# Other orders and engines for the norms, token sums, weight sums and first quad of an attention-plus-FFN kernel

## What is computed

```python
x = x + attn(layernorm(x))        # (8, 1024, 512)
x = x + ffn(layernorm(x))

# attn
c   = (x @ W_to_kv.T) @ W_compress.T              # 1024 x 64
ch  = layernorm(c) * gamma + beta
q, k, v = ch @ W_q.T, ch @ W_k.T, ch @ W_v.T      # 64 each, rope on q and k
o   = softmax(causal(q @ k.T / 8)) @ v
z   = o @ W_comp2lat.T
out = z @ W_to_kv + z @ W_out_res.T + b_out_res

# ffn
hidden = silu(x @ W1.T) * (x @ W3.T)              # 1024 x 2048
out    = fwht(hidden) @ W2.T                      # back to 512
```

## Time and profile before

| | |
|---|---|
| median of 3 runs | 2152.87 us (2150.15 to 2155.82) |
| the profiled execution | 2155.15 us, span 2153.4 us |
| mean granted clock of TensorE | 0.99 |
| TensorE busy | 2014.3 us, 94% |
| VectorE, ScalarE, GpSimd busy | 70%, 54%, 51% |
| DMA | 312.57 MB, 48.3% of 16 engines |

### The profile page before, as it was taken

The page is one execution under the profiler, slowest core; times in us unless marked ns, Lnnn a source line. Parts: engine busy times, 40 slices in busy tenths (PEclk is TensorE's granted clock), DMA queues, the critical chain, the costliest instruction groups (busy, mean ns, idle before and its releaser), DMA issues.

```text
span 2153.4 us, 32679 instructions
## 1 busy us (share of the span) xinstructions
PE 2014.3 (94%) x11862; PEld 1170.9 (54%) x11862; DVE 1503.4 (70%) x2626; ACT 1166.4 (54%) x1775; POOL 1091.7 (51%) x788
## 2 busy tenths in 40 slices
PE   6889999978999999999999999999999999999998
PEld 3534444445555656555555555556565555556665
DVE  7897878757776686866867687775868668663333
ACT  5866454454554656455555646546564465554443
POOL 2346641476554555455455545545555554555554
PEclk8999999999999999999999999999999999999999
DMA  8656346453464534725347444554347353373332
GB/s 326 221 192 221 122 137 168 140 174 135 123 147 131 174 102 126 181 90 164 111 119 186 133 138 121 129 148 154 122 124 177 99 165 98 113 166 125 116 97 89
DMA packets 267264, 312.57 MB, mean 145 GB/s; under 512 B 181344, under 2 KB 191712, under 8 KB 265312
## 3 DMA queue, kind: packets, MB, share of 16 engines
q1 hardware_dynamic: 267104, 310.48, 48.3%
HBM read 221.02 MB, written 47.19 MB: 125 GB/s over the span
## 4 chain that ended last, share of the span: by engine, by line
PE 54%; DVE 21%; issue 10%; ACT 9%; POOL 3%; DMA 2%; SPq 1%; ACTq 0%; DVEq 0%; POOLq 0%
PE PF L1121 10%; PE PF L1123 10%; PE PF L1122 10%; PE PD L1205 4%; PE PD L1207 4%; PE PD L1206 4%; DVE XS L2212 2%; DVE ring L2252 1%; DVE W2S L2238 1%; ACT L1409 1%; DVE XS L2035 1%; DMA XF<-Pl 1%; PE XY L942 1%; POOL ring L2576 1%; ACT H L1599 1%
## 5 line engine op out<-in xcount | busy, mean ns | idle before, releaser
L1121 PE MATMUL PF<-XF,WS 128*128 128x512 f16 x1778 | 678.2, 381 | 46.0 <-DVE PF L2220 17.9
L1123 PE MATMUL PF<-XF,WS 128*128 128x512 f16 x1778 | 676.1, 380 | 0.0
L1122 PE MATMUL PF<-XF,WS 128*128 128x512 f16 x1778 | 676.1, 380 | 0.0
L1205 PE MATMUL PD<-W2S,H 128*128 128x256 f16 x1456 | 397.7, 273 | 9.6 <-POOL H L2563 4.4
L1207 PE MATMUL PD<-W2S,H 128*128 128x256 f16 x1456 | 397.6, 273 | 0.0
L1206 PE MATMUL PD<-W2S,H 128*128 128x256 f16 x1456 | 397.5, 273 | 0.0
L2576 POOL TENSOR_TENSOR ring<-ring,W2S 128x512 f32<-128x512 f32 x192 | 258.7, 1351 | 122.1 <-ACT W2S L1607 121.6
L1121 PEld LDWEIGHTS PF<-XF,WS 128*128 128x128 f16 x1778 | 174.1, 98 | 214.5 <-issue 32.9
L1123 PEld LDWEIGHTS PF<-XF,WS 128*128 128x128 f16 x1778 | 174.5, 98 | 211.2 <-issue 2.5
L2563 POOL TENSOR_TENSOR H<-W2S,H 128x1024 f16<-128x1024 f32 x56 | 120.9, 2159 | 314.5 <-ACT H L1599 314.5
L1122 PEld LDWEIGHTS PF<-XF,WS 128*128 128x128 f16 x1778 | 174.8, 98 | 124.6 <-issue 5.9
(11 more groups left out here) (371 smaller groups left out, 3574.1 us busy)
## 6 DMA issues: line engine op xcount, KB each, us to landing
WS<-wscr SPq DMA_DIRECT2D x112, 896.0 KB, 5.1
W2S<-w2f SPq DMA_DIRECT2D x196, 256.0 KB, 2.7
ring<-x SPq DMA_DIRECT2D x56, 256.0 KB, 4.4
wscr<-WS SPq DMA_DIRECT2D x16, 896.0 KB, 4.5
out<-ring SPq DMA_DIRECT2D x56, 256.0 KB, 3.0
RAW<-w13t SPq DMA_DIRECT2D x16, 512.0 KB, 4.7
xraw<-xT SPq DMA_DIRECT2D x28, 256.0 KB, 4.1
XF<-w SPq DMA_DIRECT2D x13, 512.0 KB, 18.5
```

The lines of the kernel that those rows point to most:

```text
L1121: pe.matmul(bank, wh, th, start=i < 2 and j == 0, stop=False, skip_group_check=True)
L1122: pe.matmul(bank, wh, tl, start=False, stop=False, skip_group_check=True)
L1123: m = pe.matmul(bank, wl, th, start=False, stop=j == 1, skip_group_check=True)
L1205: pe.matmul(o, th, wh, start=i in (P1, P2, P5) and tp == 0 and r == 0, stop=False, skip_group_check=True)
```

## The change

Four things, with their slots. Nothing of the computed function changes.

**Constants.** Own places for two forms of the first quad's second pair, one table for all rounds of W2's sums (round 0 in sequence 0 at slot 58, rounds 1 to 7 in sequence 1, 9 slots apart), the load of the W1 and W3 forms in a sequence's first step one slot later. A new tile `first` holds three constants, 4 columns each.

```diff
+PLACE_B0 = {"A11": 3, "S3": 6}
...
-TPREP = ({48: 0, 59: 1}, {8: 2, 18: 3, 28: 4, 38: 5, 48: 6, 58: 7})
+TPREP = {58: 0, **{NH * 7 + 9 * x - 5: x for x in range(1, 8)}}
...
-FORMS_AT = {0: 1, 6: 2}
+FORMS_AT = {0: 2, 6: 2}
...
-            return PLACE_B[form] if kind else PLACE_A[form][q % 2]
+            if kind:
+                return PLACE_B0.get(form, PLACE_B[form]) if q == QF else PLACE_B[form]
+            return PLACE_A[form][q % 2]
...
-                return (p_d, d_no(q - 1 if kind else q - 2, 7))
+                return (p_d, d_no(q - 1 if kind and i else q - 2, 7))
+            if q == QF + 1 and kind == 0 and i in (1, 3):
+                return (p_u, unit_no(QF, 1 if i == 1 else 7))
```

```diff
-                if x in (0, 2):
-                    w.wait_ge(v_xf, xf_no(x // 2, 6))
+                if x < 2:
+                    w.wait_ge(v_xf, xf_no(x, 6))
...
-                        if f == 106:
+                        if f == 107:
                             load_form(s + 1, 1)
-                        if f == 108:
+                        if f == 109:
                             load_form(s + 1, 2)
...
-                        if f == 2:
+                        if f == 1:
                             load_form(s, 6)
...
-                    if k == 4 * QF + 1 and j in (0, 1):
+                    if k == 4 * QF + 3 and j in (0, 1):
                         load_form2(j)
...
+                    if 7 * k + j in TPREP:
+                        load_halves(TPREP[7 * k + j])
+                    if 7 * k + j - 8 in TPREP:
+                        store_sums(TPREP[7 * k + j - 8])
```

```diff
-                    w.wait_ge(v_t, t_no(s, i))
+                    w.wait_ge(g_x if s else v_t, t_no(s, i))
...
-                if s < 2 and f - 4 in TPREP[s]:
-                    sums_high(TPREP[s][f - 4])
+                if 7 * k + j - 6 in TPREP:
+                    sums_high(TPREP[7 * k + j - 6])
...
-                    if f == 103:
+                    if f == 104:
                         tokens_high(s + 1, 1)
-                    if f == 105:
+                    if f == 106:
                         tokens_high(s + 1, 2)
...
-                if s and f == 1:
+                if s and f == 0:
                     tokens_high(s, 6)
...
-                if k == 4 * QF + 4:
-                    parts_high(k // 2 - 1, 0)
...
+                if k > 4 * QF + 2 and k % 2:
+                    parts_high((k - 3) // 2, 3)
                 take_at(k, 2)
                 fill(k, 1)
                 if k > 4 * QF + 1 and k % 2 == 0:
                     parts_high(k // 2 - 1, 1)
-                if k > 4 * QF and k % 2 and k != 4 * QF + 3:
+                if k % 2:
+                    fill(k, 2)
+                if k > 4 * QF and k % 2:
                     parts_high(k // 2, 0)
                 if split and k > 1:
                     forms_high(h + 1, 0)
                     forms_high(h + 1, 1)
                 take_at(k, 3)
-                fill(k, 2)
+                if k % 2 == 0:
+                    fill(k, 2)
...
-                if k > 4 * QF + 1 and k % 2 == 0:
-                    parts_high(k // 2 - 1, 3)
```

```diff
-                    k = sv.mark(ve.tensor_tensor(t, t, v, ALU.mult))
+                    k = sv.mark(ve.scalar_tensor_tensor(t, t, -0.5, v, ALU.mult, ALU.mult))
...
-                k = sv.mark(ve.tensor_scalar(y.bitcast(I32), v.bitcast(I32), -0.5, 1597463007.0, ALU.mult, ALU.add))
-                sv.mark(ve.tensor_scalar(v, v, -0.5, None, ALU.mult))
-                return k
+                return sv.mark(ve.scalar_tensor_tensor(y.bitcast(I32), v.bitcast(I32), -0.5, first[:, 0:4], ALU.mult, ALU.add))
...
-                k = sv.mark(ve.tensor_scalar(st[:, 80:84], var, EPS, 2.0 ** -18, ALU.add, ALU.mult))
+                k = sv.mark(ve.scalar_tensor_tensor(st[:, 80:84], var, EPS, first[:, 8:12], ALU.add, ALU.mult))
...
-                    if f == 104:
+                    if f == 105:
                         tokens_low(s + 1, 1)
-                        tokens_sum(s + 1, 2)
-                    if f == 106:
+                    if f == 107:
                         tokens_low(s + 1, 2)
...
-                    if f == 110:
+                    if f == 111:
                         tokens_low(s + 1, 4)
-                        tokens_sum(s + 1, 6)
...
-                    if f == 2:
+                    if f == 1:
                         tokens_low(s, 6)
...
+                    if k == 4 * QF + 4:
+                        out_rows(QF - 1, 7)
                     fill(k - 1, 6)
...
                     low_part(k - 1)
+                if k and h in (14, 15):
+                    sum_c(k)
...
-                    sum_c(k)
-                    out_rows((k - 1) // 4 - 1, 2 * ((k - 1) % 4) + 1)
+                    if h not in (14, 15):
+                        sum_c(k)
+                    if k != 4 * QF + 4:
+                        out_rows((k - 1) // 4 - 1, 2 * ((k - 1) % 4) + 1)
```

```diff
+            def tokens_sum(s, i):
+
+                w.wait_ge(v_xs, tile_no(2 * s + 1, 3))
+                if t_no(s, i) > 1:
+                    w.wait_ge(g_x, t_no(s, i) - 1)
+                w.wait_ge(v_xf, xf_no(s, {1: 0, 4: 0, 2: 1, 6: 3}[i]))
+                b12, b22 = xquarter(s, 1, 0), xquarter(s, 1, 1)
+                u, v = {1: (b12, xblock(s, 0)), 4: (b22, b12), 2: (b22, xblock(s, 1)), 6: (xblock(s, 3), xblock(s, 2))}[i]
+                gp.tensor_tensor(xblock(s, i), u, v, ALU.subtract).then_inc(g_x, 1)
...
                     if j == 0:
-                        if k > 4 * QF + 2:
-                            parts_low((k - 3) // 2, 3)
                         form_sum(k // 2, 0)
-                    if j == 3 and k != 4 * QF + 3:
+                    if j == 1 and k > 4 * QF + 2:
+                        parts_low((k - 3) // 2, 3)
+                    if j == 3:
                         parts_low(k // 2, 0)
...
-                    if s < 2 and f - 2 in TPREP[s]:
-                        halves_sum(TPREP[s][f - 2])
...
+                    for i in range(4):
+                        if 7 * k + j - 2 - i in TPREP:
+                            halves_sum(TPREP[7 * k + j - 2 - i], i)
```

More of the change, by code:

```diff
@@ L146, in t_no @@
 def t_no(s, i):
-    return 4 * s + ({1: 1, 4: 2, 2: 3, 6: 4} if s else {1: 1, 2: 2, 4: 3, 6: 4})[i]
+    return 4 * max(s - 1, 0) + ({1: 1, 4: 2, 2: 3, 6: 4} if s else {1: 1, 2: 2, 4: 3, 6: 4})[i]
 def wform_no(h, part):
@@ L302, in build_kernel @@
         pbias = sb("pbias", [128, 2], F32)
+        first = sb("first", [128, 12], F32)
         XY = ctx.enter_context(nc.psum_tensor("XY", [128, 1024], F32))
@@ L1907, in norm1 @@
                 sv.after(kept["stats"])
-                k = sv.mark(ve.tensor_scalar(st[:, 44:48], var, EPS / 65536, EPS * EPS / 65536, ALU.mult, ALU.add))
+                k = sv.mark(ve.scalar_tensor_tensor(st[:, 44:48], var, EPS / 65536, first[:, 4:8], ALU.mult, ALU.add))
                 sv.after(kept["squares"])
@@ L2285, in _ @@
             ve.memset(VF[:, :, 64:128], 0.0)
+            for i, v in enumerate((1597463007.0, EPS * EPS / 65536, 2.0 ** -18)):
+                k = sv.mark(ve.memset(first[:, 4 * i:4 * i + 4], v))
+            sv.after(k)
             w.wait_ge(d_small, 16)
@@ L2415, in fill @@
                         split2(SPLIT_AT[f])
-                if s < 2 and f - 5 in TPREP[s]:
-                    sums_low(TPREP[s][f - 5])
+                if 7 * k + j - 7 in TPREP:
+                    sums_low(TPREP[7 * k + j - 7])
                 if s + 1 < NS:
@@ L2602, in product_sums @@
                     if j == 0:
-                        if k == 4 * QF + 4:
-                            parts_low(k // 2 - 1, 0)
                         form_sum(k // 2 - 1, 1)
@@ L2633, in _ @@
                             attention(2 * s + 2 + c, slot)
[L2634 to L2635 removed]
+                    if s + 1 < NS:
+                        if f == 102:
+                            tokens_sum(s + 1, 1)
+                        if f == 103:
+                            tokens_sum(s + 1, 4)
+                        if f == 105:
+                            tokens_sum(s + 1, 2)
+                        if f == 110:
+                            tokens_sum(s + 1, 6)
+                    for i in range(4):
+                        if 7 * k + j - 2 - i in TPREP:
+                            halves_sum(TPREP[7 * k + j - 2 - i], i)
                     if s == 0:
```

36 lines of the change are left out of this document (14 added, 22 removed).

## The result

The changed kernel takes 2105.68 us in the median of four runs (2104.8 to 2107.57), the kernel before, run beside it, 2153.48 (2150.15 to 2155.82): a ratio of 0.978, with a 95% interval of 0.9763 to 0.9797. It gains 47.8 us where 62.1 were forecast. The profiled execution took 2107.57 us, its span is 2105.8.

What follows compares the result with a forecast made beforehand. TensorE, busy 94% of the span, was taken to bound the kernel, other engines counting only where it waits. Terms summed to 62.1 us off 2155.15, so 2093, or about 2091 against the runs' median; range 2073 to 2124.

Steps and rivals of the forecast that it cites:

- new waits: Waits the change adds on GpSimd and the SP queue, 0 to 25 us over the kernel, taken as 8.
- Latent first: ScalarE's latent copy ahead of parts_high in odd steps removes TensorE's waits in steps 1 and 7: 13.9 us.
- `sum_c` first in steps 14 and 15: VectorE's sum_c put first there removes two TensorE waits of 1.3 us per sequence, in six sequences: 15.6 us.
- Last form a slot earlier: Token form 6 prepared a slot earlier removes a DMA wait in six first steps, plus two clock dips: 12 us.
- ScalarE's other moves: Moving parts_high(3) and the first tile's exps eases four kinds of wait: 11 us taken, between 0 and 19.
- L1205 <- ACT L1607: Sign of a wrong forecast: in step 9, unit 6 waits for ScalarE's take of unit 4, late behind exps.
- First quad: Sequence 1: pair 9's parts made in step 19, not 20, and old rows earlier remove two waits and a dip: 6.9 us.
- W2's sums: Form sums ahead of the first W2 sum, four sums spread over four slots, ease step 22's waits: 7.7 us.
- Norms: L1860 goes, 32 times; VectorE saves 24 us, none on TensorE's path outside waits already counted: nothing added.
- Token sums on GpSimd: 28 of 32 move from VectorE; GpSimd gets 59 us, hidden, but step 15 becomes full, its last sum ending late.
- rival 2: GpSimd's chain, doubled to 25 us in step 15, makes product 4 wait at seven boundaries: 2165 us, chance 0.08.
- Rival 1: Waits return elsewhere, each move passing one to what it overtakes; half the terms return: 2122 us, chance 0.23.

Runs made afterwards that it cites:

- Experiment 9: The changed kernel with sum_c back in its old place on VectorE in steps 14 and 15, token sums still on GpSimd: 2103.69 us.
- Experiment 4: The changed kernel with ScalarE's third fill of odd steps behind parts_high and the take again: 2126.57 us.
- experiment 11: experiment 1 with the even groups' second-norm root a slot earlier and GpSimd's W2 sums and parts a slot later behind their load: 2125.37 us.
- experiment 3: The changed kernel with the norms' tensor-scalars back, one instruction more per norm: 2119.04 us.
- experiment 1: The changed kernel with the token sums of sequences 1 to 7 back on VectorE: 2093.18 us.

## Why the prediction was right and where it was wrong

The sign, and the range of 2073 to 2124, held; the forecast itself, 2078 to 2104, is missed by 2 us at its upper end. That the sum came out as near as it did is in part luck: too small and too large terms cancel. The 14 us too many are not one mechanism: terms were mis-sized on both sides, and the term for new waits most of all.

- *Latent first* (13.9): right. Eleven steps fall by 1.5 us, 16.5 together (16.54 to 15.04, step 1).
- *`sum_c` first in steps 14 and 15* (15.6): the time came (six by 2.9), the reason was mostly wrong. The prediction read the cause off step 15 alone, "in step 15 sum_c (886.59) stands behind a token sum", and took it for both steps. Experiment 9 undoes the new place for 0.5 us in step 14 and nothing in step 15. In step 15 the token sum was the cause as said, and its move to GpSimd, costed as hidden, was enough by itself. In step 14 no token sum stood ahead; 1.0 of its 1.4 us belong to L1860, whose removal was costed at nothing.
- *Last form a slot earlier* (12): the DMA's wait is gone as said, and undoing it costs 18.8 us. But the first step didn't get shorter, since the next item took its place.
- *ScalarE's other moves* (11): steps 3 and 9 fall by 1.6 and 2.6, 21 us in five sequences, more than taken, and step 10 gives 10 of it back. The feared wait, "L1205 <- ACT L1607" in step 9, isn't there in sequence 3; in sequence 1 it came, 1.2 us in step 25. Experiment 4, which undoes the edit behind most of this and of the latent term, costs 20.9 of their 24.9.
- *First quad* (6.9): 5.1 us by the trace, and the two waits of 3.8 and 1.4 us were its cause as said. The medians (3.7 us) alone don't show it.
- *W2's sums* (7.7, and 1 in sequence 0): some 3. Step 22 gained its 9.3 us and sequence 0 its 1.7, but step 21 lost 7.6. The prediction named both the store's landing and "the SP queue that also carries the attention's transposes" as the risk, and set its price at 2 us; at step 21 it was the second, with the load issued 0.2 us before GpSimd was ready for it. A slot more between the load and GpSimd's sums (experiment 11) took 5.2 us off step 21.
- *Norms* (0): 13.4. The failed step is "none of it on TensorE's path outside the waits already counted". It was argued from the waits, and not from what stood behind L1860 on its engine: a hidden sum, and in step 14 an engine without a pause up to `sum_c`, so that one of the waits already counted was L1860's own. These 6 us of step 14 stand in the 17 of the `sum_c` term too, and mustn't be added to them. That the replacements would be held like the old forms was right.
- *Token sums on GpSimd* and *new waits* (-8): -12.5 from the first steps alone, and step 10's 12.9 (five by 2.0, 2.9 in sequence 1) and step 21's 7.6 behind it, in terms above. Of rival 2 the place, product 4, was right, and its half about two-input instructions too; but what was counted was GpSimd's chain (12.5 us doubled), while the chain ended 4.1 us into the step (2 to 3 were counted) and VectorE's held low parts made up the rest. The sign didn't turn, since product 4 waited 2.95 us and a dip, not 10.

Rival 1, "waits return elsewhere", is what happened to much of the gain: the steps that became shorter gained 86.2 us together, those that became longer lost 38.6, of it 13.9 in first steps, 12.9 in step 10 and 7.6 in step 21. The forecast had 70 against 8.

## What to carry to other kernels

Before moving a sum from VectorE to GpSimd, count what it does to the two-input instructions that VectorE then runs beside it: here 1.3 us saved per sum on one engine cost 2.35 on the other and 1 to 1.4 more on each low part that met it. A chain of small dependent instructions costs what GpSimd does beside it, not what it computes, so leave out instructions first, and look at what stands behind each; moving such a chain a slot either way only chose which of TensorE's feeds was late. And when several moves ease the same wait, undo each by itself, and look at each place of the wait: here two waits of one name, of 1.3 us each, had two causes, and the move made for both was worth 0.5 us at the one and nothing at the other.

## What the runs showed of the hardware that was not expected

- A dependent chain on VectorE and a stream of ready GpSimd instructions alternate one for one: 1.18 to 1.25 us for each 128x4 instruction, for as long as the stream lasts, against 0.16 alone. A chain of nine cost 5.9 us, 2.7 with one GpSimd instruction beside it.
- The form with one tensor input is held as well: the 128x4 tensor-scalar at 1091.80 took 1.24 us, 0.15 at least. So replacing tensor-scalars by scalar-tensor-tensors changed nothing in their price (14.5 and 14.4 us for 16, 13.5 and 13.3 for 32, experiment 3); only their number did.
- The hold works both ways. A token sum on GpSimd took 2.35 us in the median and up to 3.37, a form sum (L2567) in the first step 2.26 against 1.26 us at least.
- Behind the waits of 2.9 to 3.0 us in the six first steps of sequences 2 to 7 the granted clock was 0.5 (1.2 of 2.4 GHz) for 3.4 us, once for 6.8. With the wait split into 0.7 and 1.2 us (experiment 1) no first step had such a dip. In the kernel before, it stood behind two of the six first steps' waits for the form's DMA, those of 2.1 and 2.2 us, and not behind the other four, of 1.6 and 1.7 us.
